# Seams between the stages of a perceiver block: first queries and keys kept on chip, roots taken in the tail, own banks for the feed forward's input tiles, exponentials first

## What is computed

```python
# cross attention, 16 heads; per batch 32 query rows against 257 context rows of width 128
q_big = rope(einsum('bshk,hkq->bshq', (hidden_q @ Wq.T), w_kc_q))      # width 384
kv_r = rope(kv_c)
q_r = einsum('bshq,hqr->bhsr', q_big, W_qr); k_r = einsum('bld,hdr->bhlr', kv_r, W_kr)
attn = softmax(einsum('bhsr,bhlr->bhsl', q_r, k_r))
ctx = einsum('bhsd,hkd->bhsk', einsum('bhsl,bld->bhsd', attn, kv_r), w_kc_kv)
x = x + ctx.reshape(B, S, H * K) @ Wo.T
# self attention over 32 rows, 16 heads of 32; q, k, v, o are rank-64 products with weights amp*cos(phase)
# feed forward: h = (cos(ph) + sin(ph)) * sigmoid(..); two layers of
#   h = layer_norm(h + h @ ent_w @ ent_pw ..); h = layer_norm(h + sum_p (h @ path_w[p]) * mod[p])
```

## Time and profile before

| | us |
|---|---|
| median of 3 runs | 1632.79 |
| profiled execution, whole | 1631.73 |
| its span | 1629.8 |
| PE busy | 1488.6 (91%) |
| DVE busy | 1133.2 (70%) |
| ACT busy | 809.8 (50%) |
| POOL busy | 540.5 (33%) |

### The profile page before, as it was taken

The page is one execution under the profiler, slowest core; times in us unless marked ns, Lnnn a source line. Parts: engine busy times, 40 slices in busy tenths (PEclk is TensorE's granted clock), DMA queues, the critical chain, the costliest instruction groups (busy, mean ns, idle before and its releaser), DMA issues. The chain is left out here.

```text
span 1629.8 us, 26388 instructions
## 1 busy us (share of the span) xinstructions
PE 1488.6 (91%) x8136; PEld 1127.9 (69%) x8136; DVE 1133.2 (70%) x1815; ACT 809.8 (50%) x1729; POOL 540.5 (33%) x594
## 2 busy tenths in 40 slices
PE   4799999999945999999999986999898899998998
PEld 3577777777734777777777766888543478777876
DVE  6788778887525778787878772677688645555566
ACT  4566565665533555555555542555211354555554
POOL 4245333441023454545454532221242121402021
PEclk9899999999978999999999997999898899999999
DMA  4123334233348444444444424000154100000000
GB/s 152 66 86 101 103 108 132 86 99 91 107 133 272 120 122 111 111 121 110 116 114 119 106 73 169 1 0 0 65 180 140 67 1 1 1 26 1 26 26 27
DMA packets 140518, 142.21 MB, mean 87 GB/s; under 512 B 83495, under 2 KB 103079, under 8 KB 138797
## 3 DMA queue, kind: packets, MB, share of 16 engines
q1 hardware_dynamic: 138732, 132.31, 28.0%
q10 hardware_dynamic: 1728, 9.20, 1.7%
HBM read 111.98 MB, written 29.49 MB: 87 GB/s over the span
## 5 line engine op out<-in xcount | busy, mean ns | idle before, releaser
L942 ACT ACTIVATE c_e_t_high<-c_et_ps 128x512 fp32r<-128x512 f32 x128 | 76.6, 599 | 225.9 <-PE c_et_ps L1011 225.9
L820 POOL TENSOR_TENSOR c_mixed_low<-c_whole,c_mixed_high 128x512 fp32r<-128x512 f32 x64 | 95.6, 1493 | 177.7 <-ACT c_mixed_high L954 177.7
L77 DVE TENSOR_TENSOR b_rot_parts_low<-b_rot,b_rot_parts_high 128x1536 fp32r<-128x1536 f32 x64 | 135.7, 2120 | 22.4 <-ACT b_rot_parts_high L526 22.3
L1003 PE MATMUL c_sc_ps<-c_kv_t,c_q 128*128 128x257 f32 x512 | 136.6, 391 | 13.7 <-DMA c_q<-carried_queries 13.7
L843 DVE TENSOR_REDUCE c_peak<-c_sc_ps 128x2 f32<-128x514 f32 x128 | 88.5, 692 | 54.5 <-PE c_sc_ps L1003 53.6
L264 POOL TENSOR_TENSOR b_turned_raw<-b_turn_part 128x384 f32<-128x384 f32 x32 | 70.0, 2189 | 168.1 <-DVE b_key_parts_low L77 166.9
L1521 PE MATMUL f_ps<-f_right,f_left 128*128 128x512 f32 x256 | 115.8, 614 | 8.5 <-ACT f_raw L1564 6.1
L1003 PEld LDWEIGHTS c_sc_ps<-c_kv_t,c_q 128*128 128x128 f32 x512 | 99.6, 196 | 33.1 <-DMA c_q<-carried_queries 14.5
L309 DVE TENSOR_TENSOR b_rot<-b_w_qr,b_angle 128x1536 f32<-128x1536 f32 x64 | 118.6, 1853 | 0.2
L934 ACT ACTIVATE c_e<-c_sc_ps,c_peak 128x257 f32<-128x257 f32 x256 | 118.6, 474 | 0.0
L1011 PE MATMUL c_et_ps<-ident,c_e 128*128 128x128 f32 x512 | 82.4, 284 | 35.7 <-DVE c_e L850 33.8
(11 more groups left out here) (213 smaller groups left out, 3884.2 us busy)
## 6 DMA issues: line engine op xcount, KB each, us to landing
c_q<-carried_queries SPq DMA_DIRECT2D x64, 256.0 KB, 3.7
c_ends_spread<-end_weights SPq DMA_DIRECT2D x64, 256.0 KB, 4.3
carried_queries<-x SPq DMA_DIRECT2D x7, 2048.0 KB, 11.2
b_early<-early SPq DMA_DIRECT2D x15, 640.0 KB, 3.9
c_raw<-cache_t SPq DMA_DIRECT2D x64, 128.5 KB, 3.8
c_swapped<-cache_t SPq DMA_DIRECT2D x128, 64.2 KB, 3.9
f_left<-ent_in SPq DMA_DIRECT2D x16, 512.0 KB, 5.4
f_right<-ent_out SPq DMA_DIRECT2D x16, 512.0 KB, 6.3
```

The source lines that it names most:

```text
L77: return nc.vector.tensor_tensor(low, value, high.bitcast(F32), ALU.subtract)
L820: nc.gpsimd.tensor_tensor(mixed[1][:, w, :, u], whole[:, u % 2].rearrange("p (h s) -> p h s", h=H), mixed[0][:, w, :, u].bitcast(F32), ALU ...
L1003: last = nc.tensor.matmul(sc_ps[:, 2 * half + c, 0:L], q[:, u, at], kv_t[:, u], start=True, stop=True)
```

## The change

- `query_path`: the three last stores leave the block. In their place SP loads heads 0 to 13 of the queries of batches 0 and 1 into `c_q_first` (`first_queries`), ACT copies the last pair's part for these two batches straight from PSUM (eight copies of 128 x 16), and POOL rotates the context of batch 0 (`rotate_first`). `crossing.first` loads two batches in place of four.
- `cross_attention`: SP's list begins with the context of batches 2 and 3, then the three stores, then the queries of batches 2 and 3. ACT calls Exp once on one element first (`warmed`). In every step ACT has `exponential(n + 1)` ahead of `round_turned(n)`, and DVE has `normalise(n + 1)` ahead of `split_turned(n)`.
- Its tail: a square root and a reciprocal of the first 14 deviations, and the four angle operations are cut in two parts of 768 and 512 columns. `root_deviations` is gone; the last two deviations are rooted at the start of `self_attention`.
- `self_attention`: POOL's two clears stand behind the first tile's normalisation, and ACT waits for them after `take_input(0)`.
- `feed_forward`: inputs have two banks of their own, `e_input_ps`, and are turned at units 3 to 6, one each.

```diff
@@ query_path
             body(HPAIRS - 1)
-            sp.wait_ge(qc_stored, 8 * HPAIRS)
-            for v, (lo, hi) in enumerate(((0, 8), (8, 32), (32, B))):
-                sp.dma_start(q_out[:, lo:hi, 2 * S * (HPAIRS - 1):2 * S * HPAIRS], staged[:, lo:hi].rearrange("p b h s -> p b (h s)")).then_inc(last_out[v], 16)
+            sp.wait_ge(staged_out, 16 * (HPAIRS - 1))
+            crossing.first_queries(sp, q_dram)
...
+                    if isinstance(U, int) and U >= 2 * HPAIRS - 2:
+                        at = (H - 2 + ab) * S + base
+                        nc.scalar.activation(crossing.q[:, :, at:at + G], ps[:, QC_BANK + ab].rearrange("p (b s) -> p b s", b=B)[:, 0:2], ACT.Copy)
...
@@ Crossing
+    def first_queries(self, sp, q_dram):
+        for u in range(2):
+            sp.dma_start(self.q[:, u, 0:(H - 2) * S], q_dram[u, :, 0:H - 2].rearrange("d h s -> d (h s)")).then_inc(self.q_loaded[u], 16)
+
+    def last_queries(self, sp, x1, q_dram):
+        staged = x1[:, 8:16].rearrange("p t d -> p (t d)").rearrange("p (b x) -> p b x", b=B)
+        out = q_dram.rearrange("b d h s -> d b (h s)")
+        for v, (lo, hi) in enumerate(((0, 8), (8, 32), (32, B))):
+            sp.dma_start(out[:, lo:hi, (H - 2) * S:], staged[:, lo:hi]).then_inc(self.last_out[v], 16)
...
@@ cross_attention
+                    if isinstance(b, int) and b < 2:
+                        continue
+                    if isinstance(b, int) and b == 2:
                         sp.wait_ge(crossing.last_out[0], 16)
                     if isinstance(b, int) and b == BT:
                         sp.wait_ge(crossing.last_out[1], 16)
                         sp.wait_ge(crossing.last_out[2], 16)
...
+            for u in range(2, BT):
+                crossing.load(sp, u, u)
+            crossing.last_queries(sp, x1, q_dram)
             in_tiles(sp, tile)
...
+                    if more:
+                        normalise(n + 1, 1 - half)
                     split_turned(n, u, half)
...
             add_end(TILES - 1, BT - 1)
+            dve.wait_ge(rooted, 1)
+            nc.vector.reciprocal(stat[:, 1, 0:TILES - 2], stat[:, 1, 0:TILES - 2]).then_inc(inverted, 1)
             add_out(TILES - 2)
...
-                    round_turned(n, b, u, half)
                     if not (isinstance(n, int) and n == PAIRS - 1):
                         exponential(n + 1, 1 - half)
+                    round_turned(n, b, u, half)
...
+            nc.scalar.activation(scratch[:, 0:1], ident[:, 0:1], ACT.Exp).then_inc(warmed, 1)
...
             nc.scalar.activation(holo.phase, holo.phase, ACT.Sin, bias=half_pi[:], scale=-1.0).then_inc(holo_cosined, 1)
+            act.wait_ge(kept, TILES - 2)
+            nc.scalar.activation(stat[:, 1, 0:TILES - 2], stat[:, 1, 0:TILES - 2], ACT.Sqrt, bias=eps[:], scale=1.0 / D).then_inc(rooted, 1)
...
@@ self_attention
-            nc.gpsimd.memset(e_t, 0.0).then_inc(cleared, 1)
-            nc.gpsimd.memset(keys[:], 0.0).then_inc(cleared, 1)
-
             def body(i):
                 for v in range(2):
                     t = 2 * i + v
                     wait(pool, turned, t - 1)
+                    if isinstance(i, int) and v == 1:
+                        nc.gpsimd.memset(keys[:], 0.0).then_inc(cleared, 1)
+                        nc.gpsimd.memset(e_t, 0.0).then_inc(cleared, 1)
+                        pool.wait_ge(inverted_last, 1)
...
@@ feed_forward
+        input_ps = ctx.enter_context(nc.psum_tensor("e_input_ps", [P, 2, D], F32))
-        next_inputs = {0: (0, 1), 1: (2, 3)}
-        taken_inputs = {1: (0, 1), 2: (2, 3)}
+        next_inputs = {3 + u: (u,) for u in range(G)}
+        taken_inputs = {4 + u: (u,) for u in range(G)}
```

More of the change, by code:

```diff
@@ L672, in __init__ @@
         self.table = sb("c_table", [P, 2, L])
-        self.raw = sb("c_raw", [P, BT, L])
-        self.swapped = sb("c_swapped", [P, BT, L])
+        raw, swapped = sb("c_raw", [P, 2, L]), sb("c_swapped", [P, 2, L])
+        self.raw, self.swapped = ([a[:, u] for u in range(2)] for a in (raw, swapped))
+        self.q = sb("c_q_first", [P, 2, H * S])
+        self.keys = sb("c_keys_first", [P, L])
+        self.q_loaded = [sem(f"c_q_loaded{u}") for u in range(BT)]
+        self.pool_chained, self.rotated = sem("c_pool_chained"), sem("c_rotated")
         self.table_loaded = sem("c_table_loaded")
@@ L706, in cross_attention @@
         END = L - 1
+        raw_later, swapped_later = sb("c_raw_later", [P, BT - 2, L]), sb("c_swapped_later", [P, BT - 2, L])
+        crossing.raw += [raw_later[:, u] for u in range(BT - 2)]
+        crossing.swapped += [swapped_later[:, u] for u in range(BT - 2)]
         table, raw, swapped = crossing.table, crossing.raw, crossing.swapped
@@ L807, in rotate @@
                 wait(pool, mix_taken, b - BT + 1)
-                nc.gpsimd.tensor_tensor(kv_t[:, u], part[:, 0], part[:, 1], ALU.add).then_inc(rotated_, 1)
+                nc.gpsimd.tensor_tensor(kv_t[u], part[:, 0], part[:, 1], ALU.add).then_inc(rotated_, 1)
                 pool.wait_ge(rotated_, b + 1)
@@ L898, in tile @@
                         add_out(i - 2)
-                    if more:
-                        normalise(n + 1, 1 - half)
                     if j == 4 and known(i, 2):
@@ L1002, in score @@
                     at = slice((2 * half + c) * P, (2 * half + c + 1) * P)
-                    last = nc.tensor.matmul(sc_ps[:, 2 * half + c, 0:L], q[:, u, at], kv_t[:, u], start=True, stop=True)
+                    last = nc.tensor.matmul(sc_ps[:, 2 * half + c, 0:L], q[u][:, at], kv_t[u], start=True, stop=True)
                 last.then_inc(scored, 1)
@@ L1065, in _ @@
             project(TILES - 1, 1, range(H))
-def root_deviations(nc, stat, eps, name):
-    with nc.semaphore(f"{name}_rooted") as rooted, nc.semaphore(f"{name}_inverted") as inverted, nc.Block() as block:
-        @block.scalar
-        def _(act):
-            nc.scalar.activation(stat[:, 1], stat[:, 1], ACT.Sqrt, bias=eps[:], scale=1.0 / D).then_inc(rooted, 1)
-        @block.vector
-        def _(dve):
-            dve.wait_ge(rooted, 1)
-            nc.vector.reciprocal(stat[:, 1], stat[:, 1]).then_inc(inverted, 1)
-            dve.wait_ge(inverted, 1)
 def head_of(hh):
@@ L1332, in _ @@
             dve.sem_inc(kept, 1)
+            dve.wait_ge(rooted_last, 1)
+            nc.vector.reciprocal(stat[:, 1, TILES - 2:], stat[:, 1, TILES - 2:]).then_inc(inverted_last, 1)
             dve.wait_ge(weights_done, 2)
@@ L1389, in step @@
                     take_reduced(t + 1, 1 - v)
+            nc.scalar.activation(stat[:, 1, TILES - 2:], stat[:, 1, TILES - 2:], ACT.Sqrt, bias=eps[:], scale=1.0 / D).then_inc(rooted_last, 1)
             act.wait_ge(weights_done, 2)
@@ L1769, in turn_input @@
                 pe.wait_ge(normed, t + 1)
-                if u >= 2:
-                    pe.wait_ge(x_split, t - 1)
-                elif later(i):
-                    if isinstance(i, int) and i == 1:
-                        pe.wait_ge(x_split, G - 1 + u)
-                    else:
-                        pe.wait_ge(y_split, MM * (i - 1) - 1 + u)
+                wait(pe, x_split, t - 1)
                 for c in range(CD):
-                    last = nc.tensor.transpose(turn_ps[:, u % 2, c * P:(c + 1) * P], xn[:, u, c * P:(c + 1) * P], ident[:])
+                    last = nc.tensor.transpose(input_ps[:, u % 2, c * P:(c + 1) * P], xn[:, u, c * P:(c + 1) * P], ident[:])
                 last.then_inc(x_turned, 1)
```

99 lines of the change are left out of this document (53 added, 46 removed).

## The result

| | us |
|---|---|
| before, median of 7 runs beside the changed kernel | 1632.34 |
| changed kernel, median of 7 runs | 1623.13 |
| ratio | 0.9949, 95% interval 0.9931 to 0.9967 |
| its profiled execution, span | 1621.0 |

So the change wins 8.3 us by the ratio (5.4 to 11.3; the two medians differ by 9.2); forecast were 13.5. To see where, I take the same instruction in both traces and compare the distances between such marks. A first surprise falls out at once: the last store of the query stage's weights is issued at 451.46 instead of 452.96. These 1.5 us are there from the first weights store on (at 76.0 instead of 77.5 us) and stay constant; PE's granted clock from 20 to 50 us is 0.94 instead of 0.90. I take it off.

The account below looks back on a forecast made before the run. PE, busy 1488.6 of 1629.8 us, was taken as the bound, so only closing its gaps pays. The terms -7 - 4 + 5.9 - 2.3 - 1.1 - 5 = -13.5 us gave 1619.3 us, own range 1614 to 1626 (0.57).

Parts of the forecast that it names:

- Start of the scores: Between queries and cross attention: scores start at 461.6 instead of 472.56, 11.0 us earlier; 12.2 with the table load hidden.
- Seam: Between queries and cross attention: 12.2 us taken away, 5.3 given back, gain 7 us, bounds 12.2 and 3.
- these later ones shrink, [...] I leave 4 us of them: First tile of cross attention: waits for the ends after the first stall shrink, leaving 4 us.
- the later waits unchanged: Seam's lower bound: 9 us given back at the first stall, later waits as before, gain 3 us.
- the stores block the first tile: Rival, first tile: 9.5 us stall and later waits stay; seam gives 3, tail costs 2 more; 1625 us, chance 0.14.
- Exponentials first: Cross attention's steps: exponentials and their product ahead of `normalise` win 4 us, bounds 12 won and 13 lost.
- The pace of 7.25 us for PE and DVE: Cross attention: DVE's unbroken chain and PE's own time each need 7.25 us a batch, so DVE just keeps pace.
- Tail: End of cross attention: `add_out(14)` waits behind ACT's root, delaying `project(15)`; 5.9 us lost, bounds 0 and 8.
- The 1 us for a slower clock: Cross attention's tail: after a PE wait of 8.3 us, 1 us more for running at half clock.
- Roots' block and start: Roots' block and self attention's start: 2.3 us from the removed block, 1.1 from POOL's later clears, 3.4 won.
- Feed forward: Feed forward's input tiles, transposes moved into units where PE is full: 5 us won, bounds 7 and 0.
- The rival of DVE as the bound: Cross attention: DVE's serial chain sets the pace, from 7.5 us a batch; 1638 us at 7.75, chance 0.12.

Follow-up runs that it names:

- the later stores: Changed kernel with the first of the last pair's three stores ahead of the raw loads, the rest in four stores behind the ends of batches 0 to 3; 0.9947.
- roots_alone: Kernel before with only the roots in cross attention's tail and self attention's new start (POOL's clears later); 1.0023 of before.
- tail_late: Changed kernel with DVE's wait for the root and its reciprocal moved behind `add_out(14)`; 0.9928 of before.
- the three kernels above: The kernel before, the changed kernel, and the changed kernel with stores and output weights both later; ratios 1, 0.9949 and 0.9949.
- exponentials_alone: Kernel before with only the new order of exponentials and `normalise` in DVE's and ACT's lists of cross attention; 0.9977 of before.

## Why the prediction came out as it did

**Right in sign and in most terms; 3.8 us too fast.** 1623.1 lies in the forecast's own range of 1614 to 1626. By steps:

*Start of the scores.* Forecast 8.6 us behind the last weights store (461.6), measured 7.7: from ACT's last copy to PE's first score (458.74 to 459.19) are 0.45 us and not 0.84, and the small copies cost less than 0.8. The table load is hidden.

*Seam, forecast 7, measured 1.0 (-0.5 to 2.6) alone, and by the traces 2.0 (the first pair) to 4.4 (the means at batch 6).* This is the step that failed. Up to the first `c_whole` its working held: 9.5 - 0.5 = 9 of 12.2 us given back, seen 9.3 of 11.9, with the ends at 488.1 where it had 489, for the reason that it gave. What failed is "these later ones shrink, [...] I leave 4 us of them", which was to win 3.7 us back: the three later waits fell only from 7.7 to 6.5 us, since the reads of the ends took as long as before (9.6, 7.8 and 7.1 us, before 7.3, 8.9 and 7.7), and from the first `c_whole` to batch 6 it takes 53.9 us instead of 53.3. So the forecast's own lower bound of 3 ("the later waits unchanged") is nearer than its 7, and so is the rival "the stores block the first tile" with its seam of 3, though not in the 2 us more that it gave the tail. Left out besides was the query of batch 2: "two queries at 5.65 / 4 = 1.41 us" divides a row that adds up four unequal issues, 4.19 us for the first and 0.45 for each other. Here the first took 6.25 us behind 1.75 MB of stores in SP's queue and landed 0.6 us behind the last of them, and PE waited 6.9 us. That wait ended 7.9 us before the first `c_whole`, which waited for its ends; taken away by the later stores, it left the time as it was.

*Exponentials first, forecast 4, measured 3.8 alone and, by the traces, 1.2 to 2.0 in the change.* The pace of 7.25 us for PE and DVE is what the trace has (7.26), and so is the wait for the low part in the step with `add_out`. The cut from 12 to 4 was a guess and came out by luck for the part alone; that the seam would change DVE's meeting with POOL was not in it.

*Tail, forecast 5.9 lost, measured 5.9 (`roots_alone`, 22.0 us from batch 63 to `add_out(15)` against 16.1), 6.5 (against `tail_late`) and 4.9 in the change's own trace against the kernel before.* The 5.0 us of wait are right, with their mechanism. The 1 us for a slower clock is open: the last projection had 0.87 of the clock both before and after the change, and 0.80 in `roots_alone`. In the rows of the tail the load begins 0.01 us behind Sin's end and the root 0.02 us behind the load's: 1.31 us for the change of table in all. The rule of the Trainium skill ("ScalarE: Activation LUTs", section "What ACT_TABLE_LOAD costs"), 2.66 us, is not borne out here.

*Roots' block and start, forecast 3.4, seen 4.2* from `add_out(15)` to the first turned tile (3.5 in `roots_alone`).

*Feed forward, forecast 5, measured 4.6 alone (2.6 to 6.5), 4.1 by the trace.* Right in size, though its waits did not all go: 4 of 7 us moved to the transposes of `y`.

By the prediction's own signs, the pace from batch 6 to 63 went from 7.45 to 7.42 us, within its 0.15; one short wait for `e_xn_t_low` (0.8 us) is left in the feed forward, where it foresaw none. The rival of DVE as the bound fell: three batches of four run at PE's pace. Yet it holds in the fourth, and that was worth 13 us.

## What to carry to other kernels

Where a seam waits for transfers, follow the list that issues them: starting the arithmetic 12 us earlier brought 2, because the ends were asked for only behind the stores, and stores moved further back held the next ends with a wait of their own. Count the bytes too (about 19 MB in each of the three kernels above); whether they set the pace was not tested. When two engines have equal work per step, look for the one step where one of them has more, and put that surplus into the other's waits before anything else. A wait for an off-path result (here a root) belongs behind whatever the critical engine needs from the same list.

## What the runs showed of the hardware

- The order of small instructions decides whether DVE and POOL meet: the same product of DVE took 0.69 us with no product of POOL running and 0.84 or 0.95 us with 0.29 or about 0.4 us of one left; in the batch that DVE bounds, 0.15 us more in 13 tiles is 2 us in the whole.
- A store of 1 MB in rows of 256 bytes (2 MB over 64 batches and 128 partitions) takes 9.8 to 10.8 us in the four kernels with the old seam and 15.3 to 16.3 us in the five with the new one, where the first 2 MB of output weights are loaded beside it; with those loads later, 10.6 us.
- Between Sin and Sqrt on ACT a change of table took 1.31 us in all, with 0.01 to 0.02 us on either side of the load.
- Two executions of the same stage can differ by 1.5 us in the first 76 us (granted clock from 20 to 50 us 0.90 and 0.94); over fourteen traces the first weights store is issued at 75.9 to 77.9 us. The clock of that stretch does not order them all: `exponentials_alone` has 0.89 and 76.3.
